# Expert stage: stores on SyncE's queue, loops of 24 steps, and expert numbers read two a step

## The chip, the cores and the metric

The kernel runs on one core of one Trainium2 chip. The metric is the device time of one execution in microseconds (us). TensorE is the matrix engine, ScalarE, VectorE and GpSimd are the elementwise engines, and SyncE only issues transfers. In the profile they are PE (with PEld for its weight loads), ACT, DVE, POOL and SP. A name with q (ACTq, PEldq) is that engine's own sequencer, which issues transfers, loads registers, waits and branches.

## The reference

A time-mixing block, a channel-mixing block and a mixture of 32 experts work on x of 8 x 1024 tokens with 256 features, in float32. The change touches the expert stage alone:

```python
gates = sigmoid(xt @ expert_sel.T)                  # 8192 tokens x 32 experts
sel_val, sel_idx = top_k(gates, 4)
scores = relu(einsum('nd,edf->nef', xt, keys))      # 256 -> 128 for each expert
scores = scores * gate_full[:, :, None]             # zero but for the four chosen
out = einsum('nef,efv->nv', scores, values)         # 128 -> 256, summed over experts
x = x + out
```

## The kernel before

The program has two parts. The mixing part (up to about 800 us) handles sixteen tiles of 512 tokens. At its end every token's row has been scattered four times by GpSimd into `lists` in memory, sorted by expert. `lists` is cut into units of 128 rows, 288 units in all, each for one expert, and `plan_expert` says for each unit which expert it is.

The expert stage walks `lists` in 144 steps of two units (256 rows). A step i does these things, in a pipeline several steps deep:

- SyncE (`on_sync`, `rows`) loads the 256 rows of step i into one of six buffers `xr`. It may do so as soon as the buffer is free, which is when VectorE has finished step i - 6, so SyncE runs about five steps ahead of TensorE.
- TensorE (`on_tensor`) does four things in a step: `inner` (rows times keys, for the rows of step i - 2), `turn_rows` (transposes the rows of step i), `turn_sums` (transposes the sums of step i - 4), and `outer` (hidden values times `values`, for step i - 6). The expert's number is in a register, since the keys and values are picked by it. `experts_of` fills the registers: one load brings the eight numbers of four steps. It is called for `inner` with the use "keys" and for `outer` with the use "values", so there are two loads of eight numbers in every fourth step.
- ScalarE (`on_scalar`) copies four results a step out of the accumulators (`sums`, `xt_hi`, `h_hi`, `y`), and then its `store` issues the transfer of `y` (one of four buffers) to `sorted_rows` in memory.
- VectorE (`on_vector`) makes `sums`, `xt_lo` and `h_lo`, and from step 36 on does two of the gated additions to `resid` in a step (`add`).
- GpSimd (`on_gpsimd`) gathers the finished rows back by token: for each tile of 512 tokens sixteen indirect transfers of 128 rows from `sorted_rows` into `ye`, which has room for four groups of four. The sixteen of tile t may start only when all stores of the first 8 (t + 3) steps have landed. VectorE's additions wait for them, and group g of four is gathered only when the sums of group g - 4 are done.
- SyncE also loads the residual of a tile into `resid` and stores the finished tile to `out_dram`, 512 KB each, once in eight steps (`load_resid`, `store_tile`).

The first 24 batches ("the head") have their rows at places that the program computes. For these a batch is two transfers instead of one, and the engine that issues them first loads two numbers from `plan_row` or `plan_store` (`held_rows`). So in the head ScalarE issues, for each step, one register load and two stores.

All engines run their steps from code written out one step after another. SPAN is the number of steps in the body of a loop, 48: the first 48 steps stand in a row, and a loop (`Fori`) runs twice over a body of 48 steps. The mixing part has a loop too, whose body has two tiles.

Of the kernel before, what the change touches and what calls it, by code (L numbers as in the profile page):

```python
# [32 lines left out]
E, DE, TOPK = 32, 128, 4  # L33
# [10 lines left out]
SUB = BLOCK // P  # L44
# [28 lines left out]
OUT_AT = SUM_LAG + RING + HOMES[0] * WIDE  # L73
RESID_AT = OUT_AT - 20
PLAN_STEP, FIRST_RESIDS, KEYS_FIRST = 2, 14, 7
OPEN_BELOW = (UNIT - 1) / UNIT
# [1319 lines left out]
def expert_phase(nc, scope, sem, g):  # L1396
# [34 lines left out]

    SPAN = 6 * RING
    BATCHES = SPAN // WIDE
    HEAD_BATCHES = HEAD_END // FOLD
    SUM_END = SUM_LAG + 2 * NT * J
    HELD = 4
    PART_OF = P // FOLD
    assert NSTEPS % SPAN == 0 and SPAN % HELD == 0 and SPAN // RING % RESIDS == 0 and HEAD_END <= SUB * SPAN
    assert all(BATCHES % homes == 0 and HEAD_BATCHES % homes == 0 for homes in (XB, YB))
# [33 lines left out]
    def on_sync(sp):  # L1473
        def rows(b, r):
# [7 lines left out]
            else:  # L1482
                sp.dma_start(xr[:, q], lists[bass.ds(b * (FOLD * UNIT), FOLD * UNIT), :]
                             .rearrange("(p f) d -> p f d", f=FOLD)).then_inc(rows_loaded[q], 16)

        def load_resid(tile, q, nth):

            after(sp, out_stored[q], 16 * nth)
            sp.dma_start(resid[:, q], residual[bass.ds(tile * TILE, TILE), :].rearrange("(p j) d -> p j d", j=J)
                         ).then_inc(resid_loaded[q], 16)  # L1490
# [7 lines left out]
        def step(i, r, pair):  # L1498
            if r % WIDE == 0 and within(i, 0, NSTEPS):
                b = BATCHES * pair + r // WIDE  # L1500
                after(sp, x_ready, i - (XB - 1) * WIDE)
                rows(b, r // WIDE)
            for at, act_on in ((OUT_AT, store_tile), (RESID_AT, load_resid)):
                if (r - at) % RING == 0 and within(i, at, at + NT * RING):
# [9 lines left out]
        sp.wait_ge(scattered[1], 16 * (NT // 2 - 1) * J * TOPK)  # L1514
        for i in range(SPAN):
            if i == RING:
                sp.wait_ge(last_scattered, 16 * J * TOPK)
            step(i, i % SPAN, i // SPAN)
            if i == FIRST_RESIDS:
                sp.wait_ge(places_ready, 1)  # L1520
                for tile in range(RESIDS):
                    load_resid(tile, tile, 0)
        with sp.Fori(1, NSTEPS // SPAN) as pair:
            for r in range(SPAN):
                step(SPAN * pair + r, r, pair)
# [11 lines left out]
    def on_tensor(pe):  # L1537
        held = {}

        def experts_of(b, r, use):  # L1540

            n = r % HELD
            if n == 0 or (use, r) not in held:
                _, found = nc.values_load_multi_w_load_instructions(
                    plan_expert[0:1, bass.ds(b * SUB, (HELD - n) * SUB)], engines=(pe.engine,), min_val=0,
                    max_val=E - 1,
                    skip_runtime_bounds_check_because="the plan writes all of the table, bounded, ahead of its "
                                                      "semaphores")
                for m in range(HELD - n):
                    held[use, r + m] = found[m * SUB:(m + 1) * SUB]  # L1550
            return held.pop((use, r))

        def inner(i, r, pair):

            b, q = i - H_LAG, r - H_LAG
            experts = experts_of(b, q, "keys")
            pe.wait_ge(x_ready, SPAN * pair + q // WIDE * WIDE + WIDE)
# [39 lines left out]
        def outer(i, r):  # L1597

            b, q = i - Y_LAG, r - Y_LAG
            experts = experts_of(b, q, "values")  # L1600
            pe.wait_ge(h_ready, b + 1)
# [39 lines left out]
    def on_scalar(act):  # L1641
        def store(b, r):

            q = r % YB
            act.wait_ge(ycopy_ready, (b + 1) * WIDE)
            if in_head(b):
                for n, at in enumerate(held_rows(act, plan_store, b * FOLD, LIST_ROWS - FOLD * UNIT + FOLD - 1)):
                    act.dma_start(sorted_rows[bass.ds(at, UNIT, FOLD), :], y[:, q, n, :]  # L1648
                                  ).then_inc(y_stored[q], 16)
            else:  # L1650
                act.dma_start(sorted_rows[bass.ds(b * (FOLD * UNIT), FOLD * UNIT), :]
                              .rearrange("(p f) d -> p f d", f=FOLD), y[:, q]).then_inc(y_stored[q], 16)

        def step(i, r, pair):
            done = r - Y_LAG - 1
            if done % WIDE == WIDE - 1 and within(i, Y_LAG + WIDE, NSTEPS + Y_LAG + 1):
                store(BATCHES * pair + done // WIDE, done // WIDE)
            if not within(i, 0, NSTEPS + Y_LAG):
                return
            act.wait_ge(pe_step, i + 1)  # L1660
# [19 lines left out]
        for stored in x1_stored:  # L1680
            act.wait_ge(stored, 16 * NT // 2)
        for i in range(SPAN):
            step(i, i % SPAN, i // SPAN)
        with act.Fori(1, NSTEPS // SPAN) as pair:
            for r in range(SPAN):
                step(SPAN * pair + r, r, pair)
        for i in range(NSTEPS, NSTEPS + Y_LAG + 1):
            step(i, i % SPAN, i // SPAN)

    def on_vector(dve):  # L1690
# [40 lines left out]
        split_values(dve, 0, 1)  # L1731
        for i in range(SPAN):
            if i == PLAN_STEP:
# [6 lines left out]
            if i == PLAN_STEP + 2:  # L1740
                places_sorted(dve)
        with dve.Fori(1, NSTEPS // SPAN) as pair:
            for r in range(SPAN):
                step(SPAN * pair + r, r, pair)
# [66 lines left out]
```

## Time and profile before

| what | value |
|---|---|
| device time, median of 3 runs | 1264.01 us (1259.62 to 1264.49) |
| the profiled execution, its own time | 1261.35 us |
| span of that execution in the profile | 1259.5 us |
| PE busy | 1107.5 us, 88% |
| DVE busy | 1015.1 us, 81% |
| ACT busy | 752.8 us, 60% |
| POOL busy | 760.8 us, 60% |
| DMA, mean over the span | 181 GB/s |
| expert stage, first to last transposes of PE | 809.7 to 1210.8 us |
| last gather by POOL | 1252.5 us |

The busy shares are averages over two parts with different limits. In the expert stage the share of an engine tells little, because the engines wait for each other in a ring: PE makes rows, ACT copies them, a queue stores them, POOL gathers them, DVE adds them, and PE waits for DVE's other work of the same step. So the profile is read there by the starts of successive steps and tiles.

### The profile page before, as it was taken

How to read it: one execution, taken by the hardware profiler on the slowest of the kernel's cores; microseconds unless marked ns; L12 is line 12 of the kernel's file. 1: busy time of each engine (PE TensorE's matmuls, PEld its weight loads, DVE VectorE, ACT ScalarE, POOL GpSimd, SP SyncE). 2: the span in 40 equal slices, each digit the busy share in tenths (PEclk: the TensorE clock that was granted, in tenths of full speed). 3: DMA queues.
4: the chain of work that ended last, by engine and by line, in shares of the span. 5: the costliest groups of instructions: out<-in, count | busy, mean ns of one | idle time of the engine just before them, and what ended most of it. 6: DMA issues, size and time to landing. Idle time of an engine off the chain costs nothing.

```text
span 1259.5 us, 24103 instructions
## 1 busy us (share of the span) xinstructions
PE 1107.5 (88%) x6830; PEld 953.2 (76%) x6831; DVE 1015.1 (81%) x2268; ACT 752.8 (60%) x1504; POOL 760.8 (60%) x868
## 2 busy tenths in 40 slices
PE   6799999999999999999999997377799898799870
PEld 6678888788787887887787876377799898689860
DVE  3788899899899898899899885864478888678874
ACT  4467567567568567567568557444566566456550
POOL 2434377568558558668568666620077777657776
PEclk9799999999999999999999999589999999899995
DMA  9422134234224323324322128356599999899994
GB/s 342 153 85 101 39 130 141 85 110 142 96 96 146 108 79 137 102 94 145 102 87 80 65 75 350 129 181 204 160 307 348 356 356 350 292 310 360 346 315 126
DMA packets 131134, 227.55 MB, mean 181 GB/s; under 512 B 15584, under 2 KB 74976, under 8 KB 129632
## 3 DMA queue, kind: packets, MB, share of 16 engines
q1 hardware_dynamic: 82272, 121.49, 28.1%
q0 software_dynamic: 24576, 67.14, 16.1%
q10 hardware_dynamic: 24192, 37.76, 8.0%
q8 instruction: 48, 0.79, 0.3%
q14 instruction: 46, 0.38, 0.1%
HBM read 100.50 MB, written 125.83 MB: 180 GB/s over the span
## 4 chain that ended last, share of the span: by engine, by line
POOL 29%; PE 20%; issue 18%; DVE 13%; ACT 8%; DMA 7%; ACTq 3%; POOLq 1%; DVEq 0%; SPq 0%
POOL lists L1340 13%; PE ps L452 7%; POOL ye L1758 6%; DMA ye<-sorted_rows,place_of 5%; PE ps L1567 2%; POOL th_r L1383 2%; POOL rs L1294 2%; POOL xp L1370 2%; ACTq L1648 2%; DVE resid L1707 2%; PE ps L1584 2%; DVE xp L998 1%; ACT xt_hi L1666 1%; ACT y L1676 1%; DVE stats L880 1%
## 5 line engine op out<-in xcount | busy, mean ns | idle before, releaser
L1758 POOL DMA_INDIRECT ye<-sorted_rows,place_of x256 | 247.9, 968 | 176.6 <-DMA sorted_rows<-y 88.9
L1707 DVE SCALAR_TENSOR_TENSOR resid<-ye,gates,resid 128x256 f32<-128x256 f32 x256 | 123.1, 481 | 78.1 <-DMA ye<-sorted_rows,place_of 36.9
L1567 PE MATMUL ps<-keys,xt_hi 128*128 x576 | 149.7, 337 | 37.7 <-DVE xt_lo L1720 28.9
L1340 POOL DMA_INDIRECT lists<-rows_even,slot x128 | 142.8, 1115 | 46.0 <-issue 40.3
L1340 POOL DMA_INDIRECT lists<-rows_odd,slot x128 | 138.8, 1085 | 47.0 <-issue 40.3
L1663 ACT ACTIVATE sums<-ps 128x256 f32<-128x256 f32 x144 | 55.3, 384 | 170.9 <-PE ps L1609 122.7
L1567 PEld LDWEIGHTS ps<-keys,xt_hi 128*128 128x128 f32 x576 | 111.2, 193 | 48.8 <-issue 48.5
L1040 DVE TENSOR_TENSOR k_lo<-ksq,k_hi 128x512 fp32r<-128x512 f32 x128 | 117.5, 934 | 18.3 <-ACT k_hi L778 18.2
L1570 PE MATMUL ps<-keys,xt_lo 128*128 x576 | 129.9, 226 | 0.0
L769 ACT ACTIVATE kr<-ps,bias_k 128x512 f32<-128x512 f32 x128 | 86.7, 683 | 47.2 <-PE ps L452 44.5
L1570 PEld LDWEIGHTS ps<-keys,xt_lo 128*128 128x128 f32 x576 | 112.7, 196 | 0.0
L452 PE MATMUL ps<-xn1t_hi,wt_hi 128*128 128x512 f32 x256 | 104.1, 407 | 6.4 <-DVE xn1t_lo L892 4.9
L1085 DVE RECIPROCAL u<-u 128x512 f32<-128x512 f32 x32 | 106.8, 3337 | 0.0
L452 PE MATMUL ps<-xn2t_hi,wk_hi 128*128 128x512 f32 x256 | 103.8, 406 | 2.8 <-ACT kr L769 0.8
L1607 PE MATMUL ps<-values,h_hi 128*128 x288 | 94.2, 327 | 11.3 <-issue 6.1
L659 PE MATMUL ps<-k_hi,wv_hi 128*128 128x512 f32 x256 | 103.4, 404 | 0.0
L452 PE MATMUL ps<-xn2t_hi,wk_lo 128*128 128x512 f32 x256 | 101.5, 396 | 0.0
L1720 DVE TENSOR_TENSOR xt_lo<-ps,xt_hi 128x512 fp32r<-128x512 f32 x144 | 98.8, 686 | 3.2 <-ACT xt_hi L1666 2.3
L452 PE MATMUL ps<-xn2t_lo,wk_hi 128*128 128x512 f32 x256 | 101.3, 396 | 0.0
L452 PE MATMUL ps<-xn1t_hi,wt_lo 128*128 128x512 f32 x256 | 101.1, 395 | 0.0
L452 PE MATMUL ps<-xn1t_lo,wt_hi 128*128 128x512 f32 x256 | 101.1, 395 | 0.0
L661 PE MATMUL ps<-k_hi,wv_lo 128*128 128x512 f32 x256 | 100.5, 393 | 0.0
(213 smaller groups left out, 3229.3 us busy)
## 6 DMA issues: line engine op xcount, KB each, us to landing
lists<-zeros SPq DMA_DIRECT2D x18, 2048.0 KB, 10.3
xr<-lists SPq DMA_DIRECT2D x120, 256.0 KB
sorted_rows<-y ACTq DMA_DIRECT2D x120, 256.0 KB
x_sb<-in_x SPq DMA_DIRECT2D x16, 512.0 KB, 4.4
residual<-xp SPq DMA_DIRECT2D x16, 512.0 KB, 5.1
experts_raw<-in_expert_in SPq DMA_DIRECT2D x8, 1024.0 KB, 15.1
resid<-residual SPq DMA_DIRECT2D x16, 512.0 KB, 7.4
out_dram<-resid SPq DMA_DIRECT2D x15, 512.0 KB, 6.5
```

The source lines that it names most:

```text
L452: mm = pe.matmul(bank, w(k), m(k), start=n == 0, stop=n == last)
L659: pe.matmul(bank, wv_hi[:, f, c], k_hi[:, f, :], start=f == 0, stop=False, skip_group_check=True)
L661: pe.matmul(bank, wv_lo[:, f, c], k_hi[:, f, :], start=False, stop=False, skip_group_check=True)
L1040: dve.tensor_tensor(k_lo[:, m, :], ksq[:, m % KRING, :], k_hi[:, m, :].bitcast(F32), ALU.subtract).then_inc(klo_ready, 1)
L1085: dve.reciprocal(u[:, m, :], u[:, m, :]).then_inc(rden_ready, 1)
L1340: pool.indirect_dma_start(lists, bass.IndirectOffsetOnAxis(ap=slot[:, q, n:n + 1], axis=0), rows[q][:, n // TOPK, :], None).then_inc(last_ ...
L1567: pe.matmul(cols, xt_hi[:, home, c], keys[:, bass.ds(e, 1), k].rearrange("p a h w -> p (a h w)"), start=k == 0, stop=False, skip_group_che ...
L1570: mm = pe.matmul(cols[:, 0:DE], xt_lo[:, home, c], keys[:, bass.ds(e, 1), k, 0].rearrange("p a w -> p (a w)"), start=False, stop=k == KD - ...
L1607: pe.matmul(cols, h_hi[:, q % HS, c], v_hi, start=True, stop=False)
L1707: dve.scalar_tensor_tensor(acc, ye[:, j, k, :], gate, acc, ALU.mult, ALU.add).then_inc(sum_step, 1)
L1720: dve.tensor_tensor(xt_lo[:, r % XTS], ps[:, XT + r % 2, :], xt_hi[:, r % XTS].bitcast(F32), ALU.subtract).then_inc(x_ready, 1)
L1758: pool.indirect_dma_start(ye[:, j, k, :], None, sorted_rows[0:(tile + 3) * OPENED * UNIT, :], bass.IndirectOffsetOnAxis(ap=place_of[:, n:n ...
```

## The change

Three things change. The stores of `y` move from ScalarE's `step` to SyncE's, where batch i - 12 is stored (STORE_LAG is 6 + 6) right after the rows of step i are loaded. SPAN falls from 48 to 24: the first 48 steps still stand in a row, but the loop now runs four times over 24 steps. TensorE's expert numbers are loaded two at a time, for `inner` only, and stay in registers for four steps until `outer` uses them; at the start of a loop body, where none are held, `outer` loads the numbers of its first four steps by four loads.

```diff
+STORE_LAG = HOMES[0] + Y_LAG
...
-    SPAN = 6 * RING
+    SPAN = 3 * RING
-    HELD = 4
...
     def on_sync(sp):
+        def store(b, r):
+
+            q = r % YB
+            sp.wait_ge(ycopy_ready, (b + 1) * WIDE)
+            if in_head(b):
+                for n, at in enumerate(held_rows(sp, plan_store, b * FOLD, LIST_ROWS - FOLD * UNIT + FOLD - 1)):
+                    sp.dma_start(sorted_rows[bass.ds(at, UNIT, FOLD), :], y[:, q, n, :]
+                                  ).then_inc(y_stored[q], 16)
+            else:
+                sp.dma_start(sorted_rows[bass.ds(b * (FOLD * UNIT), FOLD * UNIT), :]
+                              .rearrange("(p f) d -> p f d", f=FOLD), y[:, q]).then_inc(y_stored[q], 16)
...
                 rows(b, r // WIDE)
+            if within(i, STORE_LAG, NSTEPS + STORE_LAG):
+                store(i - STORE_LAG, r - STORE_LAG)
...
-        for i in range(SPAN):
+        for i in range(2 * SPAN):
...
-        with sp.Fori(1, NSTEPS // SPAN) as pair:
+        with sp.Fori(2, NSTEPS // SPAN) as pair:
...
     def on_tensor(pe):
-        def experts_of(b, r, use):
-
-            n = r % HELD
-            if n == 0 or (use, r) not in held:
-                _, found = nc.values_load_multi_w_load_instructions(
-                    plan_expert[0:1, bass.ds(b * SUB, (HELD - n) * SUB)], engines=(pe.engine,), min_val=0,
...
-                for m in range(HELD - n):
-                    held[use, r + m] = found[m * SUB:(m + 1) * SUB]
-            return held.pop((use, r))
+        def experts_of(first, units):
+
+            _, found = nc.values_load_multi_w_load_instructions(
+                plan_expert[0:1, bass.ds(first * SUB, units)], engines=(pe.engine,), min_val=0, max_val=E - 1,
...
+            return found
...
-            experts = experts_of(b, q, "keys")
+            experts = held[q] = experts_of(b, SUB)
...
-            experts = experts_of(b, q, "values")
+            if q not in held:
+                for n in range(Y_LAG - H_LAG):
+                    held[q + n] = experts_of(b + n, SUB)
+            experts = held.pop(q)
...
     def on_scalar(act):
-        def store(b, r):
...
         def step(i, r, pair):
-            done = r - Y_LAG - 1
-            if done % WIDE == WIDE - 1 and within(i, Y_LAG + WIDE, NSTEPS + Y_LAG + 1):
-                store(BATCHES * pair + done // WIDE, done // WIDE)
```

The loops of ScalarE and VectorE change in the same way as SyncE's. Two places show what moves.

The first is TensorE at the entry of the loop's body, before. `plan_expert` is the table of expert numbers, ISA is a register operation.

```order
L1634 UNCONDITIONAL_BRANCH
L1634 ISA
L1544 TENSOR_LOAD plan_expert
L1557 REGISTER_ALU
...
L1584 MATMUL ps<-consts,xr 128x128 x4
L90 REGISTER_ALU
L1594 MATMUL ps<-consts,sums 128x128 x2
L1544 ISA
L1544 TENSOR_LOAD plan_expert
L90 REGISTER_ALU
L1607 ISA
```

And the same place now:

```order
L1593 MATMUL ps<-consts,xr 128x128 x4
L91 REGISTER_ALU
L1603 MATMUL ps<-consts,sums 128x128 x2
L1556 ISA
L1556 TENSOR_LOAD plan_expert
L1556 ISA
L1556 TENSOR_LOAD plan_expert
L1556 ISA
L1556 TENSOR_LOAD plan_expert
L1556 ISA
L1556 TENSOR_LOAD plan_expert
L91 REGISTER_ALU
```

Ahead of the first `outer` of a body there is now a run of four loads where there was one; in the steps after it, one load stands ahead of each `inner` and none ahead of `outer`.

The second is SyncE now, in the first 48 steps, where both a row batch and a store are of the head (steps 12 to 23):

```order
L1457 TENSOR_LOAD plan_row
L1479 ISA
L1479 DMA xr<-lists 64x512
L1479 ISA
L1479 DMA xr<-lists 64x512
L1457 TENSOR_LOAD plan_store
L1492 ISA
L1492 DMA sorted_rows<-y 128x256
L1492 ISA
L1492 DMA sorted_rows<-y 128x256
```

Before, the first five of these rows were all of SyncE's step, and the last five stood in ScalarE's.

In the loop's body SyncE's rows are now, around the store of a finished tile:

```order
L1483 DMA xr<-lists 128x512
L1495 DMA sorted_rows<-y 128x512
L1506 REGISTER_ALU
L1507 ISA
L1507 DMA out_dram<-resid 128x4x256
L1483 ISA
L1483 DMA xr<-lists 128x512
L1495 DMA sorted_rows<-y 128x512
```

The 512 KB of a finished tile now stand in the same queue right ahead of the rows and the store of the next step.

## Rows read from the trace of the kernel before

**Rows 1.** Page, costliest groups: busy, mean ns, idle before and its releaser.

```profile
L1758 POOL DMA_INDIRECT ye<-sorted_rows,place_of x256 | 247.9, 968 | 176.6 <-DMA sorted_rows<-y 88.9
```

**Rows 2.** Timeline of POOL's gathers: start, length, idle before and its releaser.

```profile
913.25 0.98 POOL L1758 DMA_INDIRECT ye<-sorted_rows,place_of  x1 [84.31 <-DMA sorted_rows<-y]
914.54 0.96 POOL L1758 DMA_INDIRECT ye<-sorted_rows,place_of  x1 [0.30 <-issue]
...
1079.16 0.95 POOL L1758 DMA_INDIRECT ye<-sorted_rows,place_of  x1 [0.30 <-issue]
...
1108.83 0.95 POOL L1758 DMA_INDIRECT ye<-sorted_rows,place_of  x1 [7.45 <-DVE resid L1707]
...
1233.65 0.94 POOL L1758 DMA_INDIRECT ye<-sorted_rows,place_of  x1 [0.30 <-issue]
...
1252.48 0.95 POOL L1758 DMA_INDIRECT ye<-sorted_rows,place_of  x1 [0.31 <-issue]
```

**Rows 3.** Busy time by stretch: PE, PEld, DVE, ACT, POOL, PEclk, DMA share, GB/s.

```profile
960.00:1075.00 115.00, 104.65 (x888) 100.93 (x887) 94.43 (x222) 72.72 (x179) 85.98 (x89) 1.00 1.01 353
1075.00:1110.00 35.00, 26.03 (x195) 25.17 (x194) 20.90 (x49) 15.58 (x40) 19.22 (x21) 0.85 0.86 278
```

**Rows 4.** Timeline of ACT in the head, one step.

```profile
864.58 0.38 ACT L1663 ACTIVATE sums<-ps 128x256 f32<-128x256 f32 x1 [1.58 <-issue]
...
865.60 0.62 ACT L1676 ACTIVATE y<-ps 128x512 f32<-128x512 f32 x1
866.91 0.85 ACTq L1648 DMA_DIRECT2D sorted_rows<-y  x2
867.81 0.38 ACT L1663 ACTIVATE sums<-ps 128x256 f32<-128x256 f32 x1 [1.59 <-issue]
```

**Rows 5.** Timeline of SP in the head, three windows.

```profile
806.16 11.00 SPq L1479 DMA_DIRECT2D xr<-lists  x12
...
832.57 2.93 SPq L1479 DMA_DIRECT2D xr<-lists  x4
...
844.89 2.09 SPq L1489 DMA_DIRECT2D resid<-residual  x3
```

**Rows 6.** Line 1457, loads of two numbers: ns min/median/max, first and last start.

```profile
L1457 SPq TENSOR_LOAD <-plan_row x24: 468/477/986, 805.3 to 869.4; - x24
L1457 ACTq TENSOR_LOAD <-plan_store x24: 489/494/692, 833.0 to 908.6; - x24
```

**Rows 7.** Timeline of PE, transposes of two successive steps.

```profile
1064.22 0.62 PE L1584 MATMUL ps<-consts,xr 128*128 128x128 f32 x4
...
1066.48 0.62 PE L1584 MATMUL ps<-consts,xr 128*128 128x128 f32 x4
```

**Rows 8.** Line 1544, PE's loads of expert numbers; a weight load behind one.

```profile
L1544 PEldq TENSOR_LOAD <-plan_expert x78: 333/958/2391, 812.0 to 1216.1; - x78
...
1112.28 0.19 PEld L1567 LDWEIGHTS ps<-keys,xt_hi 128*128 128x128 f32 x1 [0.31 <-issue]
```

**Rows 9.** PE's loop branches, expert and mixing; PE's first matmul behind the first.

```profile
L1634 PEldq COMPARE_BRANCH  x2: 79/3232/6385, 1075.3 to 1211.1; - x2
...
L377 PEldq COMPARE_BRANCH  x5: 76/208/239, 276.5 to 652.4; - x5
...
1082.57 0.58 PE L1567 MATMUL ps<-keys,xt_hi 128*128 x1 [6.20 <-issue]
```

**Rows 10.** Busy time of a mixing pass; DMA queues in 380:460, then 1082:1211.

```profile
370.00:463.00 93.00, 91.16 (x485) 74.03 (x484) 84.51 (x187) 61.33 (x112) 62.60 (x76) 1.00 0.32 113
...
q1 hardware_dynamic: 5472, 6.29, 22.8%
q0 software_dynamic: 1440, 3.93, 13.4%
...
q8 instruction: 11, 0.18, 0.6%
```

**Rows 11.** Chain of waits, one store's way to POOL; median landing of a tile.

```profile
1124.13 6.00 DMA sorted_rows<-y
...
out_dram<-resid SPq DMA_DIRECT2D x15, 512.0 KB, 6.5
```

More of the change, by code:

```diff
@@ L1435, in expert_phase @@
     SUM_END = SUM_LAG + 2 * NT * J
-    HELD = 4
     PART_OF = P // FOLD
-    assert NSTEPS % SPAN == 0 and SPAN % HELD == 0 and SPAN // RING % RESIDS == 0 and HEAD_END <= SUB * SPAN
+    assert NSTEPS % SPAN == 0 and SPAN // RING % RESIDS == 0 and HEAD_END <= SUB * SPAN
     assert all(BATCHES % homes == 0 and HEAD_BATCHES % homes == 0 for homes in (XB, YB))
@@ L1538, in on_tensor @@
         held = {}
-        def experts_of(b, r, use):
-            n = r % HELD
-            if n == 0 or (use, r) not in held:
-                _, found = nc.values_load_multi_w_load_instructions(
-                    plan_expert[0:1, bass.ds(b * SUB, (HELD - n) * SUB)], engines=(pe.engine,), min_val=0,
-                    max_val=E - 1,
-                    skip_runtime_bounds_check_because="the plan writes all of the table, bounded, ahead of its "
-                                                      "semaphores")
-                for m in range(HELD - n):
-                    held[use, r + m] = found[m * SUB:(m + 1) * SUB]
-            return held.pop((use, r))
+        def experts_of(first, units):
+            _, found = nc.values_load_multi_w_load_instructions(
+                plan_expert[0:1, bass.ds(first * SUB, units)], engines=(pe.engine,), min_val=0, max_val=E - 1,
+                skip_runtime_bounds_check_because="the plan writes all of the table, bounded, ahead of its "
+                                                  "semaphores")
+            return found
         def inner(i, r, pair):
             b, q = i - H_LAG, r - H_LAG
-            experts = experts_of(b, q, "keys")
+            experts = held[q] = experts_of(b, SUB)
             pe.wait_ge(x_ready, SPAN * pair + q // WIDE * WIDE + WIDE)
@@ L1641, in on_scalar @@
     def on_scalar(act):
-        def store(b, r):
[L1644 to L1652, printed above, removed]
-        def step(i, r, pair):
-            done = r - Y_LAG - 1
-            if done % WIDE == WIDE - 1 and within(i, Y_LAG + WIDE, NSTEPS + Y_LAG + 1):
-                store(BATCHES * pair + done // WIDE, done // WIDE)
-            if not within(i, 0, NSTEPS + Y_LAG):
-                return
+        def step(i, r, pair):
             act.wait_ge(pe_step, i + 1)
@@ L1681, in on_scalar @@
             act.wait_ge(stored, 16 * NT // 2)
-        for i in range(SPAN):
+        for i in range(2 * SPAN):
             step(i, i % SPAN, i // SPAN)
-        with act.Fori(1, NSTEPS // SPAN) as pair:
+        with act.Fori(2, NSTEPS // SPAN) as pair:
             for r in range(SPAN):
                 step(SPAN * pair + r, r, pair)
-        for i in range(NSTEPS, NSTEPS + Y_LAG + 1):
+        for i in range(NSTEPS, NSTEPS + Y_LAG):
             step(i, i % SPAN, i // SPAN)
@@ L1731, in on_vector @@
         split_values(dve, 0, 1)
-        for i in range(SPAN):
+        for i in range(2 * SPAN):
             if i == PLAN_STEP:
@@ L1741, in on_vector @@
                 places_sorted(dve)
-        with dve.Fori(1, NSTEPS // SPAN) as pair:
+        with dve.Fori(2, NSTEPS // SPAN) as pair:
             for r in range(SPAN):
```

## The prediction

> **What bounds the kernel now.** I read the page's costliest groups first, then the timeline of POOL from its first gather to its last, then single steps of PE, ACT and SP. The page names 256 gathers at 968 ns, with 176.6 us of idle time before them [rows 1]. The timeline shows what they mean. A gather starts 1.25 to 1.29 us after the one before it (0.95 to 0.98 of work and 0.30 of issue), the first starts at 913.25 and the last at 1252.48, and the span ends at 1259.5, which is 6.1 us behind the last one's end at 1253.43 [rows 2]. 256 gathers at 1.25 us are 320 us, and they take 340.2. So the end of the kernel is the start of the first gather, plus POOL's 320 us, plus POOL's waits, plus 6.1. A saving on any other engine counts only if it lets the first gather start sooner or takes a wait out of POOL's row.
>
> The 340.2 us split by tiles of sixteen gathers, whose starts are in the same timeline [rows 2]. From 913.25 to 1079.16 are eight tiles, 20.74 us each. From 1079.16 to 1108.83 is one tile, 29.67 us. From 1108.83 to 1233.65 are six tiles, 20.80 each. The last tile takes 19.8. The bare pace is 20.0 a tile.
>
> **The change, part by part.**
>
> *Head: the stores leave ACT.* In the head ACT sets the pace. Its `sums` start at 864.58 and again at 867.81, 3.23 us apart, with no wait for PE between: `y` ends at 866.22, and a register load and two issues end at 867.76 [rows 4]. That is 1.54 us of sequencer work in a step which is else 1.7 us of copies, closely overlapped. PE alone can do a step in 2.26 us (transposes at 1064.22 and 1066.48) [rows 7]. Now the 1.54 us go to SP. SP's own batch of the head costs 11.00 us for six, or 1.83 each, and I take 1.9 with its load of 0.48 [rows 5, 6]. So for SP's steps 12 to 23, where both are of the head, a step costs 1.9 + 1.5 = 3.4 us. For its steps 24 to 35 the rows are one issue, about 0.5 us, and a step costs 2.0. Between them stand the three residual loads, 2.1 us [rows 5]. SP comes to its step 12 at about 831.9, one register load ahead of the issue at 832.57 [rows 5]. The sum is 12 x 3.4 + 2.1 + 12 x 2.0 = 66.9 us, so batch 23 is issued by 898.8. Before, the last register load started at 908.6 [rows 6], its issues ended near 910.1, and POOL started at 913.25, so the landing takes 3.2. The first gather starts at 902.0 and not 913.25: 11 us gained.
>
> The trace has no store of the head on SP. If its issue costs what SP's own 64-partition ones do (a batch 1.9), the sum is 12 x 3.8 + 2.1 + 12 x 2.4 = 76.5 and the gain 1.5 us. If a store is 1.2 us and a row batch stays at 1.9, it is 12 x 3.1 + 2.1 + 12 x 1.7 = 59.7 and the gain 18 us. PE would allow no more than some 24. I take 11, since ACT's 1.54 is the row for the very same transfer. SP's six row buffers give it about five steps of lead, which hides 12 x (3.4 - 2.26) = 14 us for the rows nearly whole. The four `y` buffers give the stores less, so ACT will wait for a landed store around steps 14 to 24; that is inside the sum, since SP is what it waits for.
>
> *Expert numbers.* 78 loads by PE's sequencer have a median of 0.96 us and go to 2.39 [rows 8]. They come in pairs, once in four steps. PE's sequencer runs ahead of the array: it came to the loop's branch at 1075.3, and the array's last matmul before the idle time ended at 1082.57 - 6.20 = 1076.37, 1.07 us later [rows 9]. So the first of a pair shows as idle time of 0.31 us (1112.28) [rows 8], and the second, which finds less lead, as about as much or more. With 2.26 us as the step without a load [rows 7] and 20.8 / 8 = 2.6 us as the step that the tiles show, up to 0.35 us a step is at stake. The new loads bring two numbers and not eight. Bounds: the shortest load now is 0.33 us, SP's and ACT's loads of two numbers take 0.48 and 0.49 [rows 6, 8], the longest 0.99. All are under the lead of 1.07 us, so in the body they cost nothing. If they should take 0.96 each as now, a step would lose nothing in the array but the sequencer would fall behind by some tenths of a microsecond. At each body's entry four stand in a row: 4 x 0.5 against one of 0.96, so about 0.5 us a body, and I put 2 us for all.
>
> *What the steady part gains.* PE may not go at 2.26: POOL's pace of 2.5 us a step holds it through DVE's additions, and the DMA engines are full (share 1.01 at 353 GB/s from 960 to 1075) [rows 3]. A step moves 256 KB of rows, 256 KB of stores, 256 KB of gathers and 128 KB of residuals and output, 0.917 MB. At 353 GB/s that is 2.60 us, and at POOL's pace it would be 367 GB/s. So a tile can fall from 20.8 to between 20.0 and 20.8, and I take 20.5.
>
> *The loop's branch.* PE's taken branch of the expert loop took 6.385 us, and behind it the first matmul came after 6.20 us of idle time and took 0.58 instead of 0.33 to 0.38 us; the granted clock of 1075 to 1110 was 0.85, between its two levels [rows 3, 9]. POOL paid for it: 29.67 us for one tile, 9.1 over a tile of 20.6 [rows 2]. In the mixing loop the same branch took 0.21 us in median [rows 9]. A pass there has 485 matmuls on PE [rows 10]; a step of the expert stage has 20, so the old body has 960 and the new one 480. And in 80 us of the mixing loop no queue carries instructions, while in 129 us of the expert loop eleven such transfers were made on q8 [rows 10]. So a body of 485 matmuls is kept and runs again without a fetch, one of 960 is not. The new one has more register operations between its matmuls than the mixing loop: in the program's order (whose rows may hold several alike) the mixing body has 415 rows, the new one 664, the old one 1254. I count the new one as kept: three taken branches at 0.2 us instead of one at 6.4.
>
> The Trainium skill speaks against this in "Runtime: NRT & Kernel Launch", section "Instruction fetch mechanics": a taken branch whose target is not in the current window of two pages of 16 KiB waits for a fetch. By that rule each of the three branches would stall, which is the first rival below. The trace does not agree for PE's mixing loop, where no fetch was made, although 485 matmuls and 484 weight loads are 62 KB at the 64 bytes an instruction which it gives.
>
> *The sum.* Before: 8 x 20.74 + 29.67 + 6 x 20.80 = 320.4. After: 15 x 20.5 = 307.5, plus 2 for the entries: 10.9 gained. With the head's 11 that is 22 us. Last tile and tail stay at 19.8 and 6.1. Span 1259.5 - 22 = 1237.5. The profiled execution took 1261.35 and becomes 1239.4; the median of the runs is 2.7 above it, 1264.0, and becomes 1242. That is my forecast.
>
> **The rivals.**
>
> *A, the new loop body is not kept either.* Then three taken branches each cost what one does now, 9.1 us of POOL's time and about 1 us more for the four loads behind each. 1237.5 + 3 x 10 = 1267.5 in the span, 1272 in the runs, slower than before. For it: only bodies of 485 and 960 matmuls are shown, and the new one is longer than the kept one in instructions. Against it: it is much nearer to the kept one. It ends slower only if all three branches cost over 9 us; if one or two were hidden in PE's lead, the result is a gain.
>
> *B, one queue for rows, stores and finished tiles.* The store that a tile's gathers wait for stands behind the 512 KB of a finished tile, which take 6.5 us to land, and before that store took 6.0 us on a queue of its own [rows 11]. If it comes later by 1 us of POOL's time a tile, 15 tiles lose 15 us: 1252.5 in the span, 1257 in the runs. From 1.5 us a tile on nothing is left of the gain. For it: the DMA engines are full [rows 3]. Against it: the tiles at 1079.16 and 1233.65 started with the bare 0.30 of issue, so their store had landed by then [rows 2], and the finished tile is issued a whole step ahead of that store.
> The Trainium skill, "DMA: Bandwidth & Descriptors", section "Queues, rings and completion order", says that a DMA engine takes the queues that have work in turn. By that the gathers would have one rival queue and not two and land sooner, while rows and stores share one turn; it helps one side of the ring and hurts the other, and no run here shows how much.
>
> *C, SP is as slow in the head as ACT was.* The first gather then starts near 912: 1247.5 in the span, 1252 in the runs. For it: the 0.47 us of an issue in SP's head form. Against it: ACT's row for the same transfer.
>
> **How the numbers follow.** Forecast 0.62, between 1230 (head 18, tiles of 20.1) and 1250; A 0.12 at 1272; B 0.15 around 1257; C 0.11 at 1252. What this measurement can tell from no change is 0.5%, 6.3 us: faster is under 1257.7. All of the forecast and C, and half of B, are faster, and I take a little off for what I have not seen: 0.80. Within 0.5%: half of B, and A where it is partly hidden, 0.12. Slower: A in full, 0.08. The range goes from 1230 to 1262, which leaves A and a little of each end outside.
>
> **What would show it.** Right: the first gather near 902, tile starts 20.2 to 20.8 apart with none near 29, PE's taken branches under 0.5 us, loads of two numbers well under 1 us and no idle time before the weight loads behind them, ACT's head steps 2.3 us where SP is ahead and 3.4 where it is not. Wrong: a branch over 5 us (A), waits of over 1 us for a landed store at most tile starts (B), a first gather after 908 (C).

## The result, and the profile after

All times below are medians in microseconds, and a ratio stands with its 95% interval against runs of the kernel before on the same chip. Starts, lengths and spans are those of one profiled execution each: the one of before is 2.9 us under the median of its runs, the one of the change 1.5 us above.

| | before | changed |
|---|---|---|
| time | 1264.25 | 1285.12 |
| ratio | | 1.017 [1.013, 1.021] |
| span of the profiled execution | 1259.5 | 1284.9 |
| first gather starts | 913.25 | 913.68 |
| first gather's start to last gather's end | 340.2 | 365.1 |
| last gather's end to the end of the span | 6.1 | 6.1 |

The change is slower by 1.7%, and 1242 was forecast. Start, length and tail in the table show where: the 22 us expected are missing, 11 of them at the start, and POOL's own stretch is 24.9 us longer. The page has the row that answers to [rows 1]; after the bar stand the busy time, the mean and the idle time ahead:

```profile
L1753 POOL DMA_INDIRECT ye<-sorted_rows,place_of x256 | 246.9, 964 | 202.9 <-DMA sorted_rows<-y 113.1
```

A gather costs what it did, and the idle time before them grew from 176.6 to 202.9. POOL's timeline says where it stands (start, duration, and the idle time before it with what ended it); it answers to [rows 2]:

```profile
913.68 0.98 POOL L1753 DMA_INDIRECT ye<-sorted_rows,place_of  x1 [84.66 <-DMA sorted_rows<-y]
...
982.61 0.96 POOL L1753 DMA_INDIRECT ye<-sorted_rows,place_of  x1 [6.62 <-DMA sorted_rows<-y]
...
1053.41 1.10 POOL L1753 DMA_INDIRECT ye<-sorted_rows,place_of  x1 [6.81 <-DMA sorted_rows<-y]
...
1123.90 0.94 POOL L1753 DMA_INDIRECT ye<-sorted_rows,place_of  x1 [6.69 <-DMA sorted_rows<-y]
...
1195.47 0.94 POOL L1753 DMA_INDIRECT ye<-sorted_rows,place_of  x1 [6.68 <-DVE resid L1702]
```

The four are the first gathers of tiles 3, 6, 9 and 12 (counted from 0): 70.5 to 71.6 us apart, one for each pass of 24 steps. They replace the one wait of 7.45 at 1108.83 [rows 2]. The other tiles lose up to 3.4 us each against the bare pace of 20.0, most of them over 1 us: fifteen tiles take 1258.96 - 913.68 = 345.3, or 23.0 each.

PE's branch is not what stands there. These are the rows of PE's sequencer at the loop's line (minimum, median and maximum in ns, then the first and the last start), which answer to [rows 9]:

```profile
L1646 PEldq COMPARE_BRANCH  x5: 76/208/213, 952.3 to 1233.8; - x5
```

Five branches, none above 0.21 us, where one took 6.385. PE has only its first 24 steps in a row and then goes round five times over 24, with four taken branches and the last one not taken (the text of the change and the prediction gave PE the 48 steps in a row that the other engines have, so four passes and three taken branches). Its body is entered at steps 24, 48, 72, 96 and 120. What stands at an entry is in PE's timeline behind the two transposes of sums in step 72, with PEld's row beside it and the sequencer's loads from 1024 to 1030:

```profile
1025.32 0.38 PE L1603 MATMUL ps<-consts,sums 128*128 128x128 f32 x2
1028.73 0.58 PE L1619 MATMUL ps<-values,h_hi 128*128 x1 [3.02 <-issue]
```

```profile
1028.72 0.29 PEld L1619 LDWEIGHTS ps<-values,h_hi 128*128 128x128 f32 x1 [3.25 <-issue]
```

```profile
L1556 PEldq TENSOR_LOAD <-plan_expert x5: 537/749/1152, 1024.8 to 1029.2; - x5
```

Nobody is waited for ("issue"): the array stands while the sequencer goes through the four loads that the order shows ahead of the outer product. The windows around it (busy time and count of each engine, then the granted clock, the DMA engines' share and GB/s), the one behind the stand at step 96, and the one that answers to [rows 3]:

```profile
1020.00:1028.00 8.00, 4.23 (x34) 3.79 (x34) 4.04 (x10) 2.85 (x7) 6.03 (x7) 1.00 1.02 342
1028.00:1036.00 8.00, 7.27 (x39) 7.28 (x40) 3.33 (x8) 3.02 (x8) 6.17 (x7) 0.57 0.74 213
1099.00:1107.00 8.00, 7.76 (x41) 7.47 (x41) 4.03 (x10) 3.28 (x8) 6.16 (x7) 0.57 0.71 231
960.00:1075.00 115.00, 101.07 (x797) 95.69 (x798) 85.39 (x199) 64.55 (x158) 74.37 (x78) 0.96 0.94 310
```

Behind the 3 us of idle time the granted clock is 0.57, near its lower level of 1.2 GHz, and the array is busy for 7.27 us over 39 matmul records where 34 took 4.23. Behind the stands at steps 48, 72, 96 and 120 the granted clock over the next 8 us is 0.79, 0.57, 0.57 and 0.79. So from the transposes of these steps to the next ones it takes 6.05, 6.93, 6.60 and 6.88 us. The DMA engines, at 1.01 of their time in [rows 3], are at 0.94 in the mean: 1.02 ahead of the stand and 0.74 behind it.

The loads themselves, which answer to [rows 8]:

```profile
L1556 PEldq TENSOR_LOAD <-plan_expert x168: 530/728/2033, 811.5 to 1239.6; - x168
```

168 of a median of 0.73, where there were 78 of 0.96. None takes 0.48.

### The profile page after: what moved, and what is told of

Same layout as the page of the kernel before. It is cut to its first block, busy times and chain, and to the rows that moved or that the text cites. A ratio compares the mean times of both kernels' runs of the same rounds, so it can differ in the third digit from the quotient of the medians.

```text
span 1284.9 us, 24332 instructions
## 1 busy us (share of the span) xinstructions
PE 1129.4 (88%) x6830; PEld 970.4 (76%) x6831; DVE 1015.5 (79%) x2268; ACT 753.2 (59%) x1504; POOL 761.9 (59%) x868
## 4 chain that ended last, share of the span: by engine, by line
PE 30%; POOL 26%; issue 17%; DVE 13%; DMA 7%; ACT 4%; SPq 2%; POOLq 1%; DVEq 0%; ACTq 0%
POOL lists L1341 12%; PE ps L453 8%; PE ps L1576 6%; DMA ye<-sorted_rows,place_of 4%; PE ps L1593 3%; POOL ye L1753 3%; DMA sorted_rows<-y 2%; POOL th_r L1384 2%; POOL rs L1295 2%; POOL xp L1371 2%; PE ps L1619 2%; PE ps L1579 2%; PE ps L1621 2%; PE ps L1620 2%; PE ps L1603 1%
## 5 line engine op out<-in xcount | busy, mean ns | idle before, releaser
L1753 POOL DMA_INDIRECT ye<-sorted_rows,place_of x256 | 246.9, 964 | 202.9 <-DMA sorted_rows<-y 113.1
L1576 PE MATMUL ps<-keys,xt_hi 128*128 x576 | 160.2, 355 | 32.7 <-issue 17.8
L1576 PEld LDWEIGHTS ps<-keys,xt_hi 128*128 128x128 f32 x576 | 116.0, 201 | 50.6 <-issue 49.4
L1579 PE MATMUL ps<-keys,xt_lo 128*128 x576 | 132.8, 231 | 0.0
L1579 PEld LDWEIGHTS ps<-keys,xt_lo 128*128 128x128 f32 x576 | 117.7, 204 | 0.0
L1593 PE MATMUL ps<-consts,xr 128*128 128x128 f32 x576 | 94.9, 290 | 11.4 <-DMA xr<-lists 11.3
L1671 ACT ACTIVATE y<-ps 128x512 f32<-128x512 f32 x144 | 88.5, 615 | 26.0 <-DMA sorted_rows<-y 25.0
```

Of the source, the lines that this page charges most:

```text
L1576: pe.matmul(cols, xt_hi[:, home, c], keys[:, bass.ds(e, 1), k].rearrange("p a h w -> p (a h w)"), start=k == 0, stop=False, skip_group_che ...
L1579: mm = pe.matmul(cols[:, 0:DE], xt_lo[:, home, c], keys[:, bass.ds(e, 1), k, 0].rearrange("p a w -> p (a w)"), start=False, stop=k == KD - ...
L1593: mm = pe.transpose(into.rearrange("p (t f) -> p f t", f=FOLD)[:, f, :], xr[:, b % XB, f, k * P:(k + 1) * P], ident)
L1753: pool.indirect_dma_start(ye[:, j, k, :], None, sorted_rows[0:(tile + 3) * OPENED * UNIT, :], bass.IndirectOffsetOnAxis(ap=place_of[:, n:n ...
```

## The experiments

"Length" is POOL's stretch from the first gather's start to the last one's end, 340.2 before and 365.1 changed. A difference of a few us between two lengths tells little by itself, since a profiled execution can lie some us off its median; the ratios are what decides.

### One part at a time

**Loops of 24 steps alone** (`e_span`): the kernel before with the new lines of the loops.

```diff
-    SPAN = 6 * RING
+    SPAN = 3 * RING
...
-        for i in range(SPAN):
+        for i in range(2 * SPAN):
```

> The kernel before with loops of 24 steps alone (stores on ScalarE, eight expert numbers a load). Theory L (the loss is PE's loads of expert numbers: a load costs the array the same whether it brings two numbers or eight, and the run of loads at each body's entry stops the array): at an entry there is only one load for inner and one for outer, so nothing of the loss appears; the 6.4 us branch goes and takes about 9 us out of POOL's row. 1252 to 1258 us, no tile of 29 us. Theory Q (the loss is the single queue of rows, stores and finished tiles on SyncE): the same here, since the stores are on ScalarE. Theory S (short bodies themselves cost, by the entry): slower than 1264.

Measured: 1255.22, ratio 0.992 [0.989, 0.994]; length 336.3. The loads are the old ones, so an entry has one load more and no run of four. Against the profiled executions the length is 3.9 shorter and the start 1.9 earlier; the runs show 10.7 us (0.8%), since the one profiled of before is quick (1261.35, where the runs of before in this comparison have a median of 1266.88). PE's branches take 0.21 us at most here too, and no tile is above 22.5. Rival A (the body isn't kept) has fallen.

**Stores on SyncE alone** (`e_store`): loops of 48 steps, old loads.

```diff
@@ on_sync, step
                 rows(b, r // WIDE)
+            if within(i, STORE_LAG, NSTEPS + STORE_LAG):
+                store(i - STORE_LAG, r - STORE_LAG)
@@ on_scalar, step
-            if done % WIDE == WIDE - 1 and within(i, Y_LAG + WIDE, NSTEPS + Y_LAG + 1):
-                store(BATCHES * pair + done // WIDE, done // WIDE)
```

> The kernel before with the stores on SyncE alone, loops of 48 and eight numbers a load. Theory L: the first gather stays near 913, because SyncE in the head is as slow as ScalarE was, and the tile starts stay 20.8 apart: 1260 to 1268 us. Theory Q: each tile's gathers wait for a later store, at least 1 us a tile: 1279 us or more, that is nearly all of the change's loss.

Measured: 1275.89, ratio 1.0095 [1.006, 1.013]; first gather 914.27, length 353.5. Both forecasts missed: the time lies between them, with the first gather where Theory L had it and a loss that only Theory Q had. So the move costs 1%, and not through the head, where it brings and loses nothing.

**The new loads alone** (`e_load`): loops of 48 steps, stores on ScalarE.

```diff
-            experts = experts_of(b, q, "keys")
+            experts = held[q] = experts_of(b, SUB)
...
+            if q not in held:
+                for n in range(Y_LAG - H_LAG):
+                    held[q + n] = experts_of(b + n, SUB)
+            experts = held.pop(q)
```

> The kernel before with the new loads of expert numbers alone (two numbers a step, four loads at a body's entry), at loops of 48. Theory L: two entries inside the stage (steps 48 and 96) cost POOL about 6 us each over the old ones, and the loads in each step cost the array about what the old pairs did, 0.3 us a step: 1270 to 1278 us. Theory Q: 1264 or less, since the queues are as before.

Measured: 1280.82, ratio 1.014 [1.008, 1.020]; length 353.8. That is 3 us above what was expected. Its entry at step 48 has a stand of the array like those above, but the granted clock stays at 1.00 behind it:

```profile
958.90 0.38 PE L1604 MATMUL ps<-values,h_hi 128*128 x1 [2.68 <-issue]
```

```profile
959.00:967.00 8.00, 7.65 (x64) 7.33 (x65) 5.95 (x14) 4.92 (x12) 6.17 (x7) 1.00 0.75 229
```

From the transposes of step 48 it takes 5.82 us to the next ones, and POOL waits 6.56 us at tile 3 (at 983.55), as in the changed kernel. So the stand alone is enough for that wait. The three parts multiply to 0.9916 x 1.0095 x 1.0137 = 1.0147, within the interval of the whole change's 1.017. That it fits so well is luck in part, since `e_load` has two entries while POOL gathers (steps 48 and 96) and the changed kernel four. Two of three parts cost, each about as much as the third brings or more.

### The loads: the run at an entry, or one in every step

**One load at an entry** (`e_entry`): the changed kernel, where the four loads of two numbers ahead of an entry's first outer product become one of eight. Nothing else is touched.

```diff
             if q not in held:
+                found = experts_of(b, (Y_LAG - H_LAG) * SUB)
                 for n in range(Y_LAG - H_LAG):
-                    held[q + n] = experts_of(b + n, SUB)
+                    held[q + n] = found[n * SUB:(n + 1) * SUB]
```

> The changed kernel, but with one load of eight numbers at a body's entry in place of four loads of two. Theory L: the stall ahead of the first outer of a body falls from 2.5 to 3.0 us to under 1 us, and the waits of 6.6 us that POOL has every third tile fall to about 2: four of them in the steady part, 15 to 20 us: 1265 to 1272 us. Theory Q: the waits every third tile stay: 1282 to 1288 us.

Measured: 1270.51, ratio 1.004 [1.001, 1.006]; length 348.1. The same eight numbers read in one load and not in four give back 1.3% (1.017 / 1.004), 17.0 us of POOL's length, at the four entries that lie in it. It is the number of loads that is paid for, not that of numbers. PE's stands at the entries are now 0.4 to 1.1 us, and the granted clock stays at 1.00 behind three of the four (0.79 behind the one at step 120). This is the window around the entry at step 72:

```profile
1022.00:1030.00 8.00, 8.00 (x71) 7.84 (x70) 6.96 (x17) 5.31 (x15) 6.16 (x7) 1.00 0.86 277
```

POOL's wait at tile 3 is now under 2 us.

**The same with loops of 48** (`e_keep`): `e_load` with that edit.

> The kernel before with two expert numbers loaded for inner in every step and kept for outer, loops of 48, and ONE load at a body's entry. It is e_load (1.0137 of before) without the run of four. If the run of four is the whole cost of the new loads, this is 1262 to 1267 us; if a load in every step costs the array more than two in every fourth, it stays above 1270 us. From e_entry (1.0038) less e_span (0.9916) and e_store (1.0095) I expect 1.003, 1267 to 1271 us.

Measured: 1271.67, ratio 1.006 [1.004, 1.008]; length 348.9. It is just above the expected range. What is left over the kernel before, 0.6%, is the price of one load of two numbers in every step in place of two of eight in four steps. Its loads:

```profile
L1541 PEldq TENSOR_LOAD <-plan_expert x147: 533/725/2378, 811.7 to 1223.6; - x147
```

Four steps thus take 4 x 0.73 = 2.9 us of the sequencer, where before they took 2 x 0.96 = 1.9.

**Loads of eight, shared** (`e_share`): `e_span`, but the eight numbers read for the key products are kept for the outer products too, so that there is one load in four steps and not two.

```diff
-        def experts_of(b, r, use):
+        def experts_of(b, r, steps):
...
-                    held[use, r + m] = found[m * SUB:(m + 1) * SUB]
-            return held.pop((use, r))
+                    held[r + m] = found[m * SUB:(m + 1) * SUB]
+            return held[r]
```

> e_span (loops of 24, stores on ScalarE, 0.9916 of before) with one load of eight numbers in four steps for inner, kept for outer: half as many loads as in e_span and a quarter of those of the changed kernel. If what counts is the number of loads and not of numbers, PE's idle time ahead of outer goes, steps without a wait for VectorE are 2.25 us but for one in four: 1246 to 1252 us. If the numbers count, the same as e_span, 1253 to 1257 us.

Measured: 1249.88, ratio 0.9875 [0.986, 0.989], where `e_span` has 0.992 [0.989, 0.994] on another chip; length 326.9, the shortest that any kernel here reached but 7 us above 256 gathers at the bare 1.25. POOL starts 4.6 us later here than in `e_span`, but that isn't what shortens its length: `e_all` below starts at 902.23 and has 328.5. From its start at 915.96 on POOL has one idle time over 0.6 us, of 0.88. Its loads, and the stretch of [rows 3]:

```profile
L1543 PEldq TENSOR_LOAD <-plan_expert x48: 342/1024/1938, 814.3 to 1199.5; - x48
```

```profile
960.00:1075.00 115.00, 103.90 (x896) 101.28 (x894) 95.55 (x224) 73.11 (x179) 87.65 (x90) 1.00 1.01 355
```

90 gathers in 115 us, where the changed kernel made 78. A load of eight costs more than one of two in median (1.02 against 0.73, but only 0.77 in `e_mend` below) and nothing like four times as much, and 48 of them do what 168 did. So the idea of keeping what is read for four steps was good; reading it two at a time was not.

### The stores: a shared queue, or the place in SP's line

In the changed kernel and in `e_store` SP's step first issues a load of rows, which waits for `x_ready`, and then the store. The chain of waits of `e_store` ahead of a tile's first gather (start, duration, what):

```profile
984.19 6.94 DMA ye<-sorted_rows,place_of
...
991.37 0.14 DVE resid L1705
...
992.70 0.48 DVE resid L1705
...
994.15 0.70 DVE xt_lo L1718
...
995.02 0.35 SPq L1484
...
995.50 5.58 DMA sorted_rows<-y
...
1001.95 1.00 POOL ye L1756
```

The store of a finished `y` is not released by ACT, which writes `y`, but by DVE's `xt_lo`: it lets SP's row load go, and the store stands behind that. And DVE does `xt_lo` between additions (`resid`) that wait for POOL's gathers, as the first two rows show. So a late gather makes the store late on which later gathers wait.

**Store ahead of rows** (`e_first`): `e_store` with the two swapped in SP's step. Queue, engine and bytes are the same.

```diff
+            if within(i, STORE_LAG, NSTEPS + STORE_LAG):
+                store(i - STORE_LAG, r - STORE_LAG)
             if r % WIDE == 0 and within(i, 0, NSTEPS):
...
                 rows(b, r // WIDE)
-            if within(i, STORE_LAG, NSTEPS + STORE_LAG):
-                store(i - STORE_LAG, r - STORE_LAG)
```

> The kernel before with the stores on SyncE as in e_store (1.0095 of before), but each store stands ahead of its step's row load and not behind it. Theory W (a store waits in SyncE's line behind the row load, which waits for VectorE's xt_lo, which waits for a gather; so the store that the next gathers need hangs on the last gathers): the store goes out when y is copied, and most of the 12 us come back: 1262 to 1268 us, POOL's waits for landed stores under 10 us in sum against 24.7 in e_store. Theory Q (the shared transfer queue makes the store land later): nothing changes, 1273 to 1279 us.

Measured: 1265.55, ratio 1.000 [0.998, 1.002]; length 343.8. The 1% is gone. POOL's waits for stores didn't fall as far as expected (under 10 us): 20.2 us behind the first one, from 25.0 in `e_store`; those put down to DVE's additions fell from 11.0 to 6.1. What the rest of them hangs on stays open. The same place in its chain now:

```profile
952.43 0.50 ACT y L1674
...
952.95 0.05 SPq L1496
...
953.10 3.98 DMA sorted_rows<-y
957.08 0.01 issue
957.09 0.94 POOL ye L1756
```

ACT's `y` releases the store, as before the change. This parts the two causes: what costs is the order in the line. Sharing the queue, taken together with whatever ScalarE gains by the move, changes the time by no more than 0.2%. A finished tile's transfer, from 960 to 1200, lands no later for it, in 5.6 us where before it took 6.5 (the last number, in us):

```profile
out_dram<-resid SPq DMA_DIRECT2D x11, 512.0 KB, 5.6
```

The Trainium skill, "DMA: Bandwidth & Descriptors", section "Queues, rings and completion order", says that a DMA engine takes the queues with work in turn. What one queue less does to each transfer by that rule no run here shows; in the time nothing is left of it.

### The head

**ACT reads its places for four batches at once** (`e_head`): the kernel before; in the head ACT loads the eight store places of four batches in one load and not two in each step.

```diff
+            if in_head(b) and b % 4 == 0:
+                _, at = nc.values_load_multi_w_load_instructions(
+                    plan_store[0:1, b * FOLD:(b + 4) * FOLD], engines=(act.engine,), min_val=0,
...
+                for m in range(4):
+                    places[b + m] = at[m * FOLD:(m + 1) * FOLD]
```

> The kernel before with the places of the head's stores loaded by ScalarE for four batches at once (one load of eight numbers in four steps and not one of two in each). ScalarE's step in the head falls from 3.23 by three quarters of the 0.49 us load, so 22 steps give 8 us: the first gather at 905 and not 913, and the end as much sooner, 1256 to 1259 us. If what follows is bound by something else than POOL's start, the gain is lost and it is 1264.

Measured: 1254.42, ratio 0.992 [0.990, 0.995]; first gather 904.11, length 346.8. ACT's head steps, which answer to [rows 4]:

```profile
864.48 0.38 ACT L1672 ACTIVATE sums<-ps 128x256 f32<-128x256 f32 x1 [1.06 <-issue]
...
867.18 0.39 ACT L1672 ACTIVATE sums<-ps 128x256 f32<-128x256 f32 x1 [1.06 <-PE ps L1609]
```

2.70 us a step, not 3.23. The first gather comes 9.1 us sooner, and the runs are 0.8% or 10 us shorter, a little more than expected, so that the start's gain comes through whole. (The length of 346.8 doesn't speak against it: this profiled execution is 4 us above the median of its runs, and that of before 3 below.) Fewer loads on ACT alone bring 9.1 of the 11 us that moving the stores was to bring in the head.

### Together

**Shared loads and the head** (`e_all`): `e_share` with `e_head`'s edit.

> e_share and e_head together: loops of 24, stores on ScalarE with the head's places loaded for four batches at once, eight expert numbers in every fourth step kept for outer. The two gains lie in different terms (POOL's start, POOL's waits), so they add: first gather near 905, then 327 us of gathers and 6.1: span 1238 to 1242, 1239 to 1244 us. If POOL, once started earlier, gets waits for stores again, because the rows of the steady part are no faster, it is 1245 to 1250.

Measured: 1238.62 against 1265.68, ratio 0.978 [0.975, 0.981]: faster than both kernels, and the product of its parts (0.9875 x 0.9921 = 0.980). It is 0.4 us under the expected range. POOL starts where the prediction had put it, and its last gather follows without a wait:

```profile
902.23 0.98 POOL L1767 DMA_INDIRECT ye<-sorted_rows,place_of  x1 [73.35 <-DMA sorted_rows<-y]
...
1229.76 0.95 POOL L1767 DMA_INDIRECT ye<-sorted_rows,place_of  x1 [0.30 <-issue]
```

**Sixteen numbers every eighth step** (`e_all8`): `e_all` with one line changed.

```diff
-    HELD = 4
+    HELD = 8
```

> e_all with sixteen expert numbers in every eighth step in place of eight in every fourth. If a load costs by its count alone, the array loses half as often and it is the same or 1 to 3 us under e_all (POOL is nearly without waits there already). If it costs by its numbers (some 0.06 us each over a start), a load of sixteen is over 1.1 us even at rest and the array stops for longer: 0 to 3 us over e_all. Either way the loads' own durations tell which.

Measured: 1240.84, ratio 0.9805 [0.9775, 0.9835]; length 328.4 against 328.5. Half the loads (30, median 1.16) change nothing that can be told. POOL has only two waits over 0.6 us left in either kernel, none above 2.

**The change, mended** (`e_mend`): the changed kernel with its stores on SyncE and loops of 24, but the store ahead of the rows and the shared loads of eight.

> The changed kernel with two mends: on SyncE the store stands ahead of its step's row load, and the expert numbers come eight at a time, once in four steps and at a body's entry, kept for outer. Stores stay on SyncE, loops of 24. From e_first (1.000) and e_share (0.9875) I expect 0.985 to 0.990, 1247 to 1254 us. If SyncE's queue or the head is what the changed kernel also lost by, it stays above 1258.

Measured: 1251.8, ratio 0.9895 [0.985, 0.994]; first gather 912.52, length 329.9. The two edits turn 1.7% slower into 1.05% faster: they take 35.2 us out of POOL's length. Of the 13.2 us to `e_all` 10.3 are the start, since SP still does there what it did in the change. Its loads of eight have a median of only 0.77:

```profile
L1558 PEldq TENSOR_LOAD <-plan_expert x48: 332/768/1432, 813.1 to 1198.9; - x48
```

## Why the prediction was wrong

The span came out 47.4 us above the 1237.5 of the forecast: 11.7 of it is the first gather's start (902.0 forecast), 35.8 is POOL's length (329.3 forecast).

**What sets the end: right.** Of every kernel here the span is the first gather's start, POOL's length and 6.1 us, to some tenths. All effects are in the first two.

**The branch: right.** Forecast 0.2 us a branch, measured 0.21, in loops of 24 alone (`e_span`) and in the changed kernel; in loops of 48 it still took 6.7 and 6.8 (`e_load`, `e_store`). No instruction transfer on q8 stands in the trace from 960 to 1200, where the kernel before has 20 packets. By the two-page rule of the Trainium skill in "Runtime: NRT & Kernel Launch", section "Instruction fetch mechanics", each of the four taken branches would wait for a fetch; this trace does not agree. Forecast for the part was about 9 us, and `e_span` measured 0.8%, 10.7 us. Only the number of passes was wrong: PE enters its body five times, four of them while POOL gathers.

**The loads: the step that failed first.** The prediction had "All are under the lead of 1.07 us, so in the body they cost nothing", and for the entries "4 x 0.5 against one of 0.96, so about 0.5 us a body, and I put 2 us for all". (By its own figures that is 2.0 against 0.96, so 1.04 a body; why only half is taken isn't said.) Both went wrong on the price. It was taken from SP's and ACT's loads of two numbers (0.48, 0.49) and the shortest of PE's (0.33), as if fewer numbers were a shorter load. On PE one of two took 0.53 at the least and 0.73 in median, so four in a row are 2.9 us against a lead of 1.07. The array stands for 2.5 to 3.0 us, nearly the whole run, so the lead was mostly gone by then. Then came what no term held: the granted clock fell behind each of the four stands, and the step takes 6 to 7 us. The steps from 48, 72, 96 and 120 sum to 26.5 us and the ones behind them to 14.0; in `e_entry` the same eight take 15.0 and 10.5. That is 14.9 us more, of the 17.0 by which the lengths differ. Most of an entry's price is the stand: the one of `e_load` at full clock takes 5.8 us and 2.4 for the step behind it, 8.2, where `e_entry`'s four take 5.6 to 8.0 and the changed kernel's 9.5 to 10.8. So the clock is worth some 1.2 to 2.5 us an entry, an estimate from these rows. The prediction compared a load with the lead, but not the run of four with it, though it had both numbers in hand. The load in every step, put at nothing, is 0.6% (`e_keep`).

The Trainium skill has a line that spoke for this, and that the prediction did not weigh: "DMA: Bandwidth & Descriptors", section "Latency and other measured facts", gives a register load a floor of some 600 ns. An estimate by it would be 2.4 us for four in a row. The trace comes near, with a median of 0.73 for two numbers; but the shortest of them took 0.53, and a load of four numbers 0.33 [rows 8], both under that floor.

**The store's queue: the wrong mechanism of a rival.** Rival B had the place right (POOL's waits for landed stores) and a price of 1 us a tile, and reckoned it by transfer time: the store behind the 512 KB of a finished tile. `e_first` keeps that and costs nothing. What cost 1% is that the store stands behind SP's wait for a free row buffer (`x_ready`). The prediction named what each queue held, but not what SP would be waiting for when a store became ready, which the order's rows showed (row load, then store). In the changed kernel the chain reads the same:

```profile
976.80 0.66 DVE xt_lo L1715
...
977.64 0.35 SPq L1483
...
978.10 4.37 DMA sorted_rows<-y
...
982.61 0.96 POOL ye L1753
```

Without both faults (`e_mend`) POOL's length is 329.9, and the prediction's sum for it was 15 x 20.5 + 2 + 19.8 = 329.3. That it comes so near is luck in part, since 20.5 was picked between 20.0 and 20.8.

**The head: rival C came true.** 11 us were forecast and the first gather starts at 913.68. SP's timeline in the head:

```profile
831.28 8.35 SPq L1479 DMA_DIRECT2D xr<-lists  x10
840.32 0.89 SPq L1492 DMA_DIRECT2D sorted_rows<-y  x2
...
879.20 0.86 SPq L1492 DMA_DIRECT2D sorted_rows<-y  x2
...
883.02 0.86 SPq L1492 DMA_DIRECT2D sorted_rows<-y  x2
883.93 0.44 SPq L1483 DMA_DIRECT2D xr<-lists  x1
...
909.97 0.85 SPq L1492 DMA_DIRECT2D sorted_rows<-y  x2
```

The 12 us between the forecast 898.8 for batch 23 and 910.8 have three parts. The ten row issues at 831.28 are the steps 8 to 12, so step 12 begins at about 838.1 and not at 831.9: 6.2 us, a misreading of which step stands at [rows 5]'s 832.57. The trace of before had it, since the three residual loads at 844.89 are behind step 14, and the six issues right ahead of them are the steps 12 to 14:

```profile
839.84 5.00 SPq L1479 DMA_DIRECT2D xr<-lists  x6
```

Steps 12 to 23 take 45.8 and not 42.9, most of them at 3.5 to 3.8 each (879.20 to 883.02 is one), for 2.9. Steps 24 to 35 take 26.9 and not 24, at 2.25 each, which is PE's pace [rows 7], for 2.9. So SP's own issues (0.86 for two in place of ACT's) were priced nearly right and the start wrong. That ACT is held by SP's stores there shows in its waits from 840 to 912 (us in total, times, longest):

```profile
ACT y L1671 <- DMA sorted_rows<-y: 25.0, 13, 5.2
```

That SP and nothing else holds the head was not tried by itself. But the five kernels with the stores on SP start their gathers at 912.5 to 914.3, `e_mend` among them, and the five with ACT's head as before at 911.4 to 916.0: SP is as slow there as ACT was.

**The steady part: right in what is possible, wrong for this kernel.** "So a tile can fall from 20.8 to between 20.0 and 20.8, and I take 20.5": fifteen tiles of `e_share` take 20.5 each and of `e_mend` 20.7. The changed kernel has 23.0, for the two reasons above.

## What to carry to other kernels

Count a sequencer's register loads and not what they bring, and hold every run of them, at a loop's entry above all, against the lead that the sequencer has over its array; here one wide load, kept and shared, beat narrow ones. Before a transfer is moved to another engine's line, read what that engine waits for just ahead of the new place, and who that releaser itself waits for: a free queue is no help behind a foreign wait. A loop that has to be short enough to be kept gains by that alone, but has more entries, so whatever an entry does is multiplied.

## What the chip showed beside this

- A register load's time on PE hardly follows its size. At the least it took 0.53 us for two numbers and 0.59 for eight. Loads of four, the first of a body and of the steps behind the loop, took from 0.33 (before, behind the branch of 6.4 us) to 0.98 (`e_share`, at the entry of step 48). The medians of kernels that read mostly two, eight and sixteen are 0.70 to 0.73, 0.77 to 1.02, and 1.16, and the longest loads take 1.4 to 2.4 us. Why one of two is never as short as the shortest of four stays open.
- Behind the stands of 2.5 to 3.0 us of the changed kernel the granted clock was 0.57 to 0.79 over the next 8 us, after 0.90 to 1.00 in the 8 before. That isn't so each time: behind the one of 2.68 us in `e_load` it stayed at 1.00. Behind stands of 0.4 to 1.1 us at the same steps (`e_entry`) it was 1.00 three times and 0.79 once.
- A body of 480 matmuls is kept on PE (0.21 us a taken branch, no packet on q8 from 960 to 1200), one of 960 is not (5.6 to 7.1 us in six kernels, 20 or 21 packets).
